# Two attentions in a one-core Trainium2 kernel: the lead phases without their extra product per score item

## The reference, cut to what matters

```python
# layer 0
attn = jnp.einsum('bqc,bkc->bqk', q * scale, k)
attn = (attn.reshape(-1, WS, WS, WS, WS) + rel_h[:, :, :, :, None] + rel_w[:, :, :, None, :]).reshape(-1, N, N)
attn = jax.nn.softmax(attn, axis=-1)
out = attn @ v
...
# layer 3
att = jnp.einsum('bhqd,bhkd->bhqk', q, k) * scale
att = jax.nn.softmax(att, axis=-1)
y = jnp.einsum('bhqk,bhkd->bhqd', att, v)
```

## Time and profile before

| | |
|---|---|
| median of three runs | 1116.69 us (1114.40 to 1118.52) |
| profiled execution | 1116.58 us, of which the span of instructions is 1114.7 us |
| mean granted TensorE clock | 0.931 of full speed |
| TensorE busy | 991.8 us, 7510 products |
| VectorE busy | 578.7 us |
| ScalarE busy | 419.9 us |
| lead phase of `l0a` | first score at 110.59 us of the span, first `score_t` at 126.07 us |
| lead phase of `l3a` | first score at 882.39 us, first `score_t` at 893.51 us |

### The profile page before, as it was taken

How to read it: one execution, slowest core, us unless ns; L and a number is a source line. 1 busy time by engine, 2 the same in 40 slices (tenths; PEclk the granted TensorE clock), 3 DMA queues, 4 the chain that set the end, 5 groups by cost and what they waited for, 6 DMA issues and landing times. The chain is left out here.

```text
span 1114.7 us, 20465 instructions
## 1 busy us (share of the span) xinstructions
PE 991.8 (89%) x7510; PEld 752.8 (68%) x7511; DVE 578.7 (52%) x1396; ACT 419.9 (38%) x853; POOL 282.8 (25%) x397
## 2 busy tenths in 40 slices
PE   5998999999699999999799469999959799993996
PEld 5796888887375887787698426666647445572675
DVE  3844755552321565655666733444368477744221
ACT  3755254545223242444350011111127266641332
POOL 4663401010200121100001334555412211103242
PEclk9976999999899999999898679999969899995998
DMA  5455753310011320000007311112144433415760
GB/s 93 105 156 154 183 145 81 92 44 2 3 43 64 89 48 1 23 1 1 1 2 215 106 36 43 51 46 50 31 135 107 125 117 90 144 44 186 206 207 13
DMA packets 103318, 91.58 MB, mean 82 GB/s; under 512 B 25905, under 2 KB 95095, under 8 KB 102590
## 3 DMA queue, kind: packets, MB, share of 16 engines
q1 hardware_dynamic: 93221, 77.20, 25.2%
q0 software_dynamic: 5632, 11.07, 3.7%
q10 hardware_dynamic: 4377, 2.12, 0.7%
HBM read 64.44 MB, written 29.70 MB: 84 GB/s over the span
## 5 line engine op out<-in xcount | busy, mean ns | idle before, releaser
L1358 DVE TENSOR_REDUCE l0a_nmax<-l0a_psS 98x2 f32<-98x392 f32 x96 | 54.3, 566 | 40.8 <-PE l0a_psS L1175 32.8
L2904 ACT ACTIVATE l2e_H<-l2e_psH 128x512 f32<-128x512 f32 x40 | 21.7, 594 | 130.3 <-PE l2e_psH L2866 130.3
L921 ACT ACTIVATE l3a_PT<-l3a_psST 128x512 f32<-128x512 f32 x96 | 54.6, 595 | 31.8 <-PE l3a_psST L832 31.1
L1308 ACT ACTIVATE l0a_PT<-l0a_psST 98x392 f32<-98x392 f32 x96 | 47.2, 497 | 42.2 <-PE l0a_psST L1217 41.8
L2884 PEld LDWEIGHTS l2e_psY<-W2T,l2e_HT 128*128 128x128 f32 x320 | 51.4, 190 | 16.1 <-issue 15.9
L2827 POOL DMA_INDIRECT ys<-l2e_Y,result_of x40 | 42.0, 1050 | 72.4 <-DVE l2e_Y L2931 66.3
L2884 PE MATMUL l2e_psY<-W2T,l2e_HT 128*128 x320 | 57.3, 332 | 1.5 <-DVE l2e_Y L2931 0.8
L967 DVE TENSOR_REDUCE l3a_nmax<-l3a_psS 128x2 f32<-128x512 f32 x48 | 33.0, 687 | 25.0 <-PE l3a_psS L802 25.0
L2931 DVE COPY l2e_Y<-l2e_psY 128x384 f32<-128x384 f32 x20 | 11.2, 558 | 65.4 <-PE l2e_psY L2884 65.4
L2863 PE MATMUL l2e_psH<-W1T,l2e_XT 128*128 x80 | 41.3, 640 | 2.8 <-issue 2.0
L2822 POOL DMA_INDIRECT l2e_X<-xn,token_at x40 | 39.2, 980 | 17.2 <-issue 17.2
(11 more groups left out here) (591 smaller groups left out, 2698.6 us busy)
## 6 DMA issues: line engine op xcount, KB each, us to landing
l3w_A<-in_w SPq DMA_DIRECT2D x8, 771.0 KB, 4.7
l3w_B<-in_w SPq DMA_DIRECT2D x8, 672.0 KB, 5.5
l3a_QS<-qd SPq DMA_DIRECT2D x72, 64.0 KB, 2.2
l3a_KS<-kd SPq DMA_DIRECT2D x72, 64.0 KB, 2.3
rd<-l0r_p SPq DMA_DIRECT2D x24, 168.0 KB
first_QS<-qd SPq DMA_DIRECT2D x54, 64.0 KB
first_KS<-kd SPq DMA_DIRECT2D x54, 64.0 KB
W2T<-in_w2t SPq DMA_DIRECT2D x2, 1536.0 KB, 16.5
```

What stands on the lines that cost most here:

```text
L921: nc.scalar.activation(PT[n % 3][:, s, :], psST[item % 2][:, :], ACT.Exp).then_inc(exp_done, 1)
L1308: ex = nc.scalar.activation(PT[n % 3][0:WQ, s, :], psST[item % 2][0:WQ, 0:2 * W0], ACT.Exp)
L1358: mx = nc.vector.tensor_reduce(nmax[k % 2][0:WQ, 2 * j:2 * (j + 1), s], psS[item % 2][0:WQ, 0:2 * W0].rearrange("p (t k) -> p t k", t=2), ...
```

## The change

The product behind each score item of the lead phase is taken out in both attentions, 24 in `l0a` and 16 in `l3a`. The function `fill` stays defined and is no longer called. Nothing is put in its place, and the streams of the other four engines hold the same instructions in the same order.

```diff
@@ -885,8 +885,6 @@
             for n, s in steps():
                 if scored(n):
                     score(n + lead, s)
-                    if n < 0:
-                        fill(n + lead)
                 if exped(n):
                     score_t(n, s)
                 if exped(n - 1) and s % 2:
@@ -1275,8 +1273,6 @@
             for n, s in steps():
                 if scored(n):
                     score(n + lead, s)
-                    if n < 0:
-                        nc.tensor.matmul(psB[:, 0:P], G["ident"][0:CH, :], G["QF"][:, 0, 0:P], start=True, stop=True)
                 if exped(n):
                     score_t(n, s)
                 if exped(n - 1) and s % 2:
```

## The result

The changed kernel took 1155.05 us (median of four runs: 1130.77, 1145.48, 1164.62 and 1666.78), against 1116.24 for the kernel before (1114.40 to 1118.52). The ratio is 1.0194, with an interval of 1.0146 to 1.0242; it is made from the two shortest runs, since it leaves out runs far above the shortest, so it understates the loss. The prediction was 1118.8, in a range to 1123.0: slower by 2.1 us, where it is some 39. A later set of six more runs of the same kernel gave 1130.09, 1137.21, 1146.77, 1158.07, 1166.56 and 1167.67. No run came near 1116.

What follows compares the result with a forecast made beforehand. TensorE was taken to bound the window attention's dense part, a loop through VectorE the leads. Full-clock gain -0.45, low clock +1.8 (window) and +0.9 (full attention): +2.25 on 1116.6 gave 1118.8 us, range 1115.0 to 1123.0.

Steps and rivals of the forecast that it cites:

- What bounds the kernel: Window attention's dense part: TensorE, busy all 8 us from 126 to 134; lead phases: mainly the loop through VectorE.
- The full-clock terms: Both lead phases with the clock kept full: -0.45 us in the window attention, 0 in the full one.
- The rival of -9.5 us: Both leads: the extra products are on the path, saving 5.8 and 3.7 us, so 1107.1 us; chance 0.02.
- The fall of the clock in both leads: Without extra products the clock falls at 115 in the window lead and near 886 in the full attention's.
- The rule on idle gaps: Both leads: only idle gaps of microseconds drop the clock, so it stays full, 1116.1 us; that rival's chance 0.22.
- The cost per lead item: Window lead at the low clock: an item takes 0.82 us, +0.21; full attention's lead: 0.755, +0.155.
- the upper end: Window attention's low-clock cost at most: 11 us of lead and 4 us of dense part low, +4.8 us.
- The step that failed: Window attention behind its lead: 0 to 4 us of the dense part run low, losing half their time.
- the slower rival: Clock falls in both leads and is still low when the dense parts start: +6.9, 1123.5 us; chance 0.13.
- a clock low in long stretches of the dense parts: Dense parts of the attentions: a sign that would show the prediction wrong; no size given.
- The full attention: Fall near 886: +0.5 us in its lead, +0.4 in its dense part, in all +0.9, ends 0 and +2.5.

## Why the prediction was wrong

- What bounds the kernel: right. TensorE bounds the dense part of the window attention; that is why its clock is worth so much.
- The full-clock terms (-0.45 in the window attention, 0 in the full one): not separable. The seven runs with half of the products and the clock kept have a median of 1115.59, those with bf16 products 1116.2, beside 1116.2 to 1116.4 for before. Such medians can't show half a microsecond, but a gain of several, as if the window's products were on the path, would show. The rival of -9.5 us is out.
- The fall of the clock in both leads: right, at 112.4 and 931.6 in the profiled run (forecast 115 and near 886, which is 931.3 when moved by the 45.3 us that the window attention lost before it). The rule on idle gaps that the Trainium skill gives ("TensorE: Matmul & The Clock Gate", section "Why this matters for your kernels") would have had 1116.1; here the trace disagrees with it as the only condition, since the longest wait of TensorE before the fall at 112.4 is 0.85 us. The same page of the Trainium skill, section "A second HAM failure mode: psum-queue depth-cycling", on short pauses between groups of products, points the right way for this lead. The fall at 586 shows that pauses aren't needed for one.
- The cost per lead item: right. 0.775 apart against my 0.82. The lead lost 3.4 instead of 1.35 (first `score_t` 18.9 us behind the first score, not 16.8). That is above the 2.8 that the upper end gave the lead, because the clock fell at 112.4 and not at 115, and all of the 16.4 us behind it ran low.
- The step that failed: "before the rise at 104.8 lay 4 us in which line 504 ran dense at the low clock", from which I put 0 to 4 us of the dense part at the low clock. The step takes from that one line that dense work brings the clock back within 4 us. Line 504 is a float32 product 512 columns wide on 96 rows. The attention's dense part is as dense by TensorE's busy time and didn't do the same: 96 us of it ran low and lost 42.6, that is 0.44 of each microsecond, close to the half that I reckoned. So the rate was right, the mechanism of the slower rival was right, and its duration was too short by more than twenty times. The prediction named "a clock low in long stretches of the dense parts" as a sign of being wrong, and it is the one that came. The trace of before could have warned. It had two kinds of busy stretch at the low clock: line 504, at which the clock rose, and the products of line 479, 112 and 16 columns wide, with which it stayed at 0.50 from 72 to 84 us while TensorE read busy all of the time.
- The full attention: +2.1 (+2.4 by the runs with this part alone) against +0.9, near the upper end of that term, 2.5. Its lead lost 0.2 (11.3 instead of 11.1), where I had 0.5, and the part behind it 1.9, where I had 0.4. There the dense part does bring the clock back, after 14 to 17 us.

What stays open: the run of 1666.78 us at a mean clock of 0.547. A mean of 0.547 between the levels 1.0 and 0.5 means that nine tenths of the execution ran low. Even the whole window attention at the low clock explains some 80 us (an estimate). It came once in 10 runs of the changed kernel, and in none of the 62 of before or the 87 of the other kernels; no profile of it exists. Also open is why the two attentions differ in bringing the clock back, why some turnings bring it back and others not, and which property of the extra product holds it: rows, width and spacing were not varied one by one.

## What to carry to other kernels

A product that nobody reads can hold the clock, and most of its worth here was not in its own stage but in the long stretch behind it that didn't bring a lost clock back. When judging a change that thins TensorE's work, look first for the longest TensorE-bound stretch behind it and ask what in that stretch would raise the clock; where nothing in the trace shows the same kind of product raising it, take all of the stretch as the bound of the cost. And run such a kernel more than four times: kernels near the edge had runs at 1115 and at 1163.

## What the runs showed of the hardware

- The clock of a stretch depended on the clock with which it began: the same dense work of the window attention ran 140 us at 1.00 when it began so (in the kernel with four wide products) and 86 us at 0.50 when it began low (in the changed kernel).
- The same extra products hold a full clock (before, 1116) and don't bring back a lost one (kept in the last 12 items only, 1150 to 1168).
- With 24 extra products on 96 rows none of 62 runs of before is above 1123.52; with the same columns at the same place on 32 rows none of 5 is below 1149.71. There the items also stand 0.89 apart at the full clock instead of 0.63, so rows and spacing are not told apart.
- With two float32 products of 512 columns on 128 rows behind the thin lead, all 11 runs lie at 1128.12 or below; without them all 15 runs (of the changed kernel and of its window part alone) lie at 1130.09 or above. In the profiled run the clock came back at 133.6.
- In the eight profiles with a lost clock and no wide products, it came back 1.3 to 3.9 us behind the start of a turning through the identity on 128 rows.
